# Fifteen products of zeros in place of seven on TensorE ahead of the first loads of a two-layer sequence kernel

## The reference

```python
rkv = x @ W_rkv + b_rkv                  # 512 -> 3 * 512
r, k, v = split(rkv);  r = sigmoid(r);  k = exp(k);  kv = k * v
u1, u2 = scan of kv and of k along the tokens, decay lam = exp(-exp(nu_log))
a = (u1 + gamma * kv) / (u2 + gamma * k + 1e-6) * r
x = layernorm(x + a @ W_o + b_o)
xr, xk = mu * x + (1 - mu) * x_prev      # mu_r and mu_k
r = sigmoid(xr @ W_r.T);  k = square(relu(xk @ W_k.T))
x = layernorm(x + r * (k @ W_v.T))
```

## Time and profile before

| | us |
|---|---|
| median of 3 runs | 2542.32 |
| lowest and highest of them | 2540.78, 2545.28 |
| the profiled execution | 2542.95 |
| its span, first to last instruction | 2541.2 |
| TensorE busy in it | 2509.6 |
| VectorE busy in it | 2099.5 |
| ScalarE, GpSimd busy in it | 1270.9, 1252.2 |

### The profile page before, as it was taken

One profiled execution on the slowest core, in us unless ns is written; L12 is line 12 of the kernel. 1 busy time (PEld: TensorE's weight loads), 2 busy tenths in 40 slices (PEclk: granted clock), 3 DMA queues, 4 the chain that ended last, 5 costly groups with the idle time before them and its releaser, 6 DMA issues.

```text
span 2541.2 us, 32904 instructions
## 1 busy us (share of the span) xinstructions
PE 2509.6 (99%) x11255; PEld 2075.1 (82%) x11255; DVE 2099.5 (83%) x2693; ACT 1270.9 (50%) x2157; POOL 1252.2 (49%) x1130
## 2 busy tenths in 40 slices
PE   8999999999999999999999999999999999999998
PEld 6788888878888788888888878888888878888877
DVE  8888888878888788887888888888888888888884
ACT  5544455544455354554545544455444555444555
POOL 5744445444454445545455444544444454545544
PEclk9999999999999999999999999999999999999999
DMA  4001101111011110101111111101111111110100
GB/s 178 17 34 50 51 34 36 44 39 51 34 45 39 35 51 34 50 34 35 50 46 38 34 35 50 50 34 34 35 50 50 34 39 31 49 51 34 49 27 34
DMA packets 57791, 110.73 MB, mean 44 GB/s; under 512 B 7041, under 2 KB 7041, under 8 KB 57089
## 3 DMA queue, kind: packets, MB, share of 16 engines
q1 hardware_dynamic: 56736, 108.03, 12.3%
q10 hardware_dynamic: 864, 0.28, 0.1%
HBM read 74.73 MB, written 33.55 MB: 43 GB/s over the span
## 4 chain that ended last, share of the span: by engine, by line
PE 94%; issue 2%; POOL 2%; DVE 1%; ACT 0%; DMA 0%; POOLq 0%; DVEq 0%
PE bankB L1193 13%; PE bankB L1194 13%; PE bankB L1195 13%; PE bankA L1173 13%; PE bankA L1172 13%; PE bankA L1174 13%; PE bankB L1240 4%; PE bankB L1242 4%; PE bankB L1241 4%; PE bankB L1218 2%; POOL xk_lo L449 0%; DVE att_f L939 0%; POOL wk_lo L412 0%; DMA wrkv_f<-in_w_rkv 0%; POOL att_f L422 0%
## 5 line engine op out<-in xcount | busy, mean ns | idle before, releaser
L1173 PE MATMUL bankA<-x_lo,wrkv_hi 128*128 128x512 f32 x1488 | 580.3, 390 | 14.5 <-issue 14.5
L1172 PE MATMUL bankA<-x_hi,wrkv_hi 128*128 128x512 f32 x1488 | 584.3, 393 | 3.5 <-POOL x_lo L417 3.5
L1174 PE MATMUL bankA<-x_hi,wrkv_lo 128*128 128x512 f32 x1488 | 580.4, 390 | 0.0
L923 DVE RECIPROCAL gate<-gate 128x512 f32<-128x512 f32 x128 | 429.2, 3353 | 4.4
L422 POOL TENSOR_TENSOR att_f<-att_f,gate 128x512 f32<-128x512 f32 x128 | 207.1, 1618 | 276.0 <-DVE att_f L944 276.0
L1174 PEld LDWEIGHTS bankA<-x_hi,wrkv_lo 128*128 128x128 f32 x1488 | 280.0, 188 | 74.1 <-issue 15.7
L1172 PEld LDWEIGHTS bankA<-x_hi,wrkv_hi 128*128 128x128 f32 x1488 | 280.2, 188 | 62.3 <-POOL x_lo L417 3.9
L1173 PEld LDWEIGHTS bankA<-x_lo,wrkv_hi 128*128 128x128 f32 x1488 | 280.2, 188 | 57.6 <-issue 0.5
L449 POOL TENSOR_TENSOR xk_lo<-xk_f,xk_hi 128x512 fp32r<-128x512 f32 x124 | 178.8, 1477 | 241.2 <-ACT xk_hi L707 241.2
L699 ACT ACTIVATE z<-z,shift,rstd 128x512 f32<-128x512 f32 x124 | 94.3, 808 | 356.7 <-POOL shift L442 356.7
L920 DVE SCALAR_TENSOR_TENSOR gate<-u,gate 128x512 f32<-128x512 f32 x128 | 182.9, 1429 | 104.2 <-ACT gate L647 101.8
(11 more groups left out here) (160 smaller groups left out, 5607.6 us busy)
## 6 DMA issues: line engine op xcount, KB each, us to landing
y<-in_x SPq DMA_DIRECT2D x128, 256.0 KB, 2.7
x_f<-in_xT SPq DMA_DIRECT2D x124, 256.0 KB, 4.0
out<-z SPq DMA_DIRECT2D x124, 256.0 KB, 2.1
wrkv_f<-in_w_rkv SPq DMA_DIRECT2D x3, 768.0 KB, 9.2
xk_f<-in_xT SPq DMA_DIRECT2D x4, 256.0 KB, 5.6
wo_f<-in_w_o SPq DMA_DIRECT2D x1, 1024.0 KB, 12.4
wr_f<-in_w_r SPq DMA_DIRECT2D x1, 1024.0 KB, 14.9
wv_f<-in_w_v SPq DMA_DIRECT2D x1, 1024.0 KB, 16.7
```

Source lines behind the costliest of these rows:

```text
L923: dve.reciprocal(gate[:, c % 2], gate[:, c % 2]).then_inc(rec_made, 1)
L1172: pe.matmul(bank[:], w_hi, hi[:, h], start=(h == 0), stop=False)
L1173: pe.matmul(bank[:], w_hi, lo[:, h], start=False, stop=False)
L1174: last = pe.matmul(bank[:], w_lo, hi[:, h], start=False, stop=(h == NC - 1))
```

## The change

The constant WARM is 15 in place of 7. TensorE issues fifteen products of zeros ahead of its first group, and the two waits for `columns_written` ask for fifteen. The instructions of the other engines and their order are the same, and TensorE's behind the products of zeros are too.

```diff
-WARM = 7
+WARM = 15
```

## The result

The changed kernel took 2523.74 us at the median, the kernel before 2544.0 us in the same comparison: a ratio of 0.9921, 95% interval 0.9908 to 0.9935. That is 0.8% faster, where 0.1% was forecast and everything beyond 0.2% had been given 0.03. The profiled execution took 2523.07 us, with a span of 2521.3 against 2541.2: 19.9 us less. One of the six runs of the changed kernel took 6672.16 us, for a reason that no trace shows; the ratio is taken without it, and the median of the other five is 2523.38.

The account below looks back on a forecast made before the run. TensorE, busy 99% of the span, was taken as the bound. An early start worth 2.24 us at no cost took 2542.95 to 2540.7, or 2540.1 us by the median; range 2537.4 to 2543.2.

Parts of the forecast that it names:

- The start: First 18 us: fifteen zeros raise TensorE's clock before real work, so the first twelve real products finish 2.31 us earlier.
- the second group: TensorE's second group of twelve real products near the start: begins at 10.77 us instead of 13.08.
- the key's exponential: ScalarE's first key exponential: starts at 11.04 us, 2.24 earlier than 13.28, once the decay constants are done.
- the gate's: ScalarE's gate exponential in the first block, waiting for TensorE's second group: at 13.7 us instead of 16.02.
- VectorE's long step: First-block step at 17.49 us, waiting for gate and key: moves 2.24 us earlier, to near 15.3.
- GpSimd's step: Where the chain passes from VectorE to GpSimd, at 55.4 us: moves to 53.2.
- its own terms: Allowances around 2540.1 us: 0.3 for the cost's bounds, 0.9 for the loads, 2.2 for half the run spread.
- The second clock stretch: Seven slow TensorE products after the idle stretch before 50.84 us: expected again; no gain if the clock stayed up.
- the waits for the low keys: TensorE waiting on GpSimd's low keys around 93 us: about 0.6 us in all, expected to remain.
- Nothing else is moved: Claim that eight more zero products on TensorE's line move nothing else; their cost, hidden by the load wait, is nothing.
- After that TensorE is full: Claim that behind the low-key waits around 93 us TensorE has no idle time, so 2.24 us arrive at the end.
- The rival of more than 0.2% faster: A gain of over 5.1 us, against 3.9 held by all slow products at the start and later; chance 0.03.

Follow-up runs that it names:

- E1: The kernel before, with its seven zero products written as three float32 ones and one float32r, the same instruction count but longer work: 2541.94 us.
- e4: The kernel before, seven zero products, plus an instruction at the head of TensorE's loop announcing the branch back: 2524.74 us.
- e12: The kernel before, seven zero products, with TensorE's loop head set by hand at slot 224 of its 256-instruction block: 2524.89 us.
- e7: The kernel before, seven zero products, with TensorE's loop head set by hand at slot 239 of its 256-instruction block: 2533.52 us.
- e9: The changed kernel's fifteen zero products plus the announcement of the branch at the head of TensorE's loop: 2522.15 us.
- e11: The changed kernel, fifteen zero products, with TensorE's loop head put by hand at slot 239 of its block: 2530.57 us.
- e8: The changed kernel plus twelve unused products in TensorE's idle stretch ahead of the second block's fourth input: 2523.86 us.
- e10: The kernel before with nine zero products instead of seven, plus the announcement of the branch in TensorE's loop: 2524.86 us.
- e2: The kernel before plus eight zero products of 16 columns behind its seven; part of VectorE's sums is lost from the result: 2525.62 us.
- e3: The kernel before with ten zero products instead of seven: 2523.87 us.
- e6: The kernel before plus eight zero products of 16 columns ahead of its seven, so the result is whole: 2524.04 us.
- e5: The kernel before with nine zero products instead of seven: 2548.4 us.

## Why the prediction was wrong

**The start: right, term by term.** The zeros were to end by 7.4 and ended at 6.88; TensorE was to be at the second group at 10.77 and was at 10.79, though its first real product started 0.09 late; the key's exponential at 11.04 (10.99), the gate's at 13.7 (13.71), VectorE's long step near 15.3 (15.17), GpSimd's step at 53.2 (53.11, from 55.39: 2.28 earlier, where 2.24 was the sum). The clock held over the idle stretch of 1.11 us that was left. E1 gives the price of this part alone in the time: 1.8 us by the medians (2543.77 - 2541.94), within the noise. That 2.28 came so near to 2.24 is in part luck: in other traces of kernels with the old seven zeros (e4, e12, e7) the clock rises elsewhere and GpSimd's step comes at 54.51, 54.62 and 55.90, in those with fifteen (after, e9, e11) at 53.06 to 53.14, so that the early start is worth 1.4 to 2.8 us from one pair to another; the prediction had estimated 1.0 to 2.6. By its own terms (0.3, 0.9 and 2.2 around 2540.1) its range would reach from 2537.9 to 2543.5, not from 2537.4 to 2543.2; neither comes near 2523.74.

**The second clock stretch: right in kind.** The clock fell again, for eight products in place of seven, and e8 shows that keeping it up brings nothing here: TensorE waits for GpSimd's low keys instead.

**A further 1.04 us** lie between 55 and 208 us (3.32 - 2.28). Of this the prediction had nothing. In the kernel before, the keys of the first block took 12.07 us with the waits for the low keys (91.18 to 103.25), after 10.88 (89.05 to 99.93) without any: GpSimd's chain came 3.4 us earlier to the low keys (84.91 in place of 88.30), and in e7, whose GpSimd step at 55.90 is later than that of the kernel before, they took 10.88 too. So this wait comes and goes without the change: with the old start it is there in one kernel and not in the other. The prediction had it stay; what decides it is open.

**The failed step** is the sentence on which the cost rests: "Nothing else is moved". That was true of the order of the instructions and false of their place. Sixteen instructions ahead of the loop shift every later one in the blocks in which they are fetched, and with that the six stops at the branches back go, and the fall of the clock behind one of them: 16.50 of the 19.9 us, which the sum had put at nothing. The second fault made it invisible: "After that TensorE is full" rested on a stretch from 100 to 500 us, and the first stop is at 520. The row with 14.5 us and "issue" was the largest wait of TensorE in the trace. The rival of more than 0.2% faster was priced by the slow products alone, 3.9 us at most, and got 0.03; with that row on the table its ceiling would have been 3.9 + 17.5.

The Trainium skill has the mechanism. Its page Runtime: NRT & Kernel Launch, section "Instruction fetch mechanics", says that instructions come in blocks of 16 KiB, 256 of them, and that a taken branch whose target isn't held breaks the prefetch and waits for a transfer. The block's size agrees with the packets of 16.4 KB and with the stop at seventeen instructions in e7, and the wait at the branch with its records of 3.3 to 3.9 us. But this wait isn't the one that the time shows: TensorE works on through it, and what it stands still for is the block behind the target's, which is fetched only then.

## What to carry to other kernels

In a long loop like this one the sequencer pays at every branch back, and how much of it the engine feels hangs on how much work lies before it then and on where the loop's first instruction lies in a block: here from nothing to 3.9 us a turn, decided by code that has nothing to do with the loop. Before trusting a comparison of two kernels that differ by a few instructions ahead of a loop, list the waits with no releaser on the engine that is full, and compare the length of a turn in both; a difference there belongs to the place, not to the edit. Announce the branch, or set the place well inside a block, and the loop stops depending on its surroundings.

## What the runs showed of the hardware

- One weight load and one product more ahead of the loop moved the time by 24.5 us (2548.4 to 2523.87 us), and the time isn't monotone in their number: 7, 9, 10 and 15 zero products give 2544.0, 2548.4, 2523.87 and 2523.74.
- The branch back holds TensorE's sequencer for 3.3 to 3.9 us and, announced, for 0.34 to 0.39. The other engines' records of their branches in the kernel before last 0.04 to 0.06 us.
- The announcement saves eleven packets of 16.4 KB. It removes the stops, but against a good place it brings nothing that these traces can tell: with it a turn took 311.75 to 312.11 us (e4, e9, e10), without it and without stops 311.75 to 312.25 (after, e2, e3, e6, e12).
- A stop of 2.0 to 3.3 us can be followed by a stretch at the lower clock level, eight or nine products long and worth 1.6 us. It came behind 6 of the 18 stops of before, e1 and e5, and behind none of the 12 of e7 and e11, which were 0.6 to 1.5 us long. In the kernel before it came behind a stop of 2.28 us and not behind those of 2.82 and 2.73.
- Products of zeros raise the clock. In e12 seven did it too (granted clock 1.00 from 4.5 to 7.8), but it was down again (0.50) when the first real product started at 7.92. Fifteen at the lower level would have taken 6.8 us (0.59 + 13 x 0.426 + 0.63) and took 5.41. In the changed kernel it held over 1.11 us of idleness, in e1 over 1.55. In e3, behind 1.98 us, the first products ran 0.23 us apart, then eight 0.43 apart. So a clock that is up at the first product can still fall a little later.
